# Second expert pair's down weights, and one chunk of the first pair's, loaded as each home comes free

## The chip, the cores and the metric

The kernel runs on one core of a Trainium2 chip. The metric is the device time of one execution in microseconds, lower is better; the time before is the median of three runs.

## The reference

The program is a two-layer graph network on 384 nodes with 1024 features, all in float32. Each layer adds the results of two attention-like mixers to x, normalises, and then adds a mixture of eight experts. The change is in the last stage, the experts of the second layer:

```python
aff = feats @ centroids.T
eid = jnp.argmax(aff, axis=1)
xhat = (feats - mu) * jax.lax.rsqrt(var + EPS)
for e in range(8):
    mask = (eid == e).astype(feats.dtype)[:, None]
    h = xhat * gamma[e] + beta[e]
    y = feats + jax.nn.relu(h @ w1[e] + b1[e]) @ w2[e] + b2[e]
    alpha = jax.nn.sigmoid(feats @ centroids[e])[:, None]
    out = out + mask * (alpha * y + (1.0 - alpha) * feats)
```

Here `w1[e]` is 1024 by 512 and `w2[e]` is 512 by 1024: 2 MB each, 32 MB for eight experts. Each of the 384 rows goes to one expert.

## The kernel before

**Pairs and chunks.** The last stage runs the eight experts as four pairs, 0 to 3; each expert of a pair has 64 of the 128 columns. A pair has sixteen weight chunks of 512 KB (128 partitions of 4 KB): eight up chunks (w1) and eight down chunks (w2). Chunk r of a kind belongs to expert r // 4 of the pair and to step j = r % 4, so step j needs chunks j and 4 + j. `up_pair(i)` (L1573 to L1595, matmuls at L1591) and `down_pair(i)` (L1597 to L1615, matmuls at L1610) work in the four steps j = 0 to 3. TensorE's order is: up of pair 0, up of pair 1, down of pair 0, up of pair 2, down of pair 1, up of pair 3, down of pair 2, the first half of the adding up of results (`spread`, L1630), down of pair 3, and the second half of the adding up. Rows of pairs 1 to 3 are fetched by indirect DMAs (L593) from `xs`, to which ScalarE stores the features (L684); they are turned at L1569. The rows of pair 0 come from SBUF by a matmul with a 0/1 matrix, the first pair's row selection (L1536). The results of pairs 0 and 1 go to `ys` (stored at L862) and come back by three indirect DMAs, and VectorE adds them at L2060. The bias rows b2 of each pair are two broadcast loads (L913).

**Homes.** SBUF is full, so chunks go to tensors that earlier work has finished with. Each of the lists `w1_even`, `w2_even` (pairs 0 and 2), `w1_odd`, `w2_odd` (pairs 1 and 3) names eight homes. Those of `w2_odd` are: three thirds of `Y[:, 3]`, which hold the normalised features of row blocks 0, 1 and 2 and are read last by the first pair's row selection; three thirds of `xnT` (`flat[2]`), which hold the turned features and are read last by the affinity matmuls at L1504, after which the semaphore `pe_output` stands at AFF2; and two thirds of `Y[:, 2]`, which hold the attention's result and are read last by the last matmuls at L1026, after which `chunk_used` stands at CH_F1. The home of chunk 7 of pair 0's down weights is `rows[:, 0]`, which holds a row of factors that VectorE reads last at L2273, just ahead of the L2277 that counts `x2_done` up.

**The order of loads.** SyncE (SP) issues all weight loads from one program, in order: an instruction behind a wait is issued only when the wait is over. Behind the up chunks of pair 1 (into `ring`) it waits for `xn_ready` at 4 * NB (VectorE's L2232, the last of its kind), issues chunk 7 of pair 0's down weights, waits for the row selection (`M1s.xt_ready` at 2) and for the gathered rows of pair 1 (`odd_gathered`), and issues all eight down chunks of pair 1. Behind them come the up chunks of pair 2 (each step's two wait for the same step of pair 0's up), those of pair 3 (wait for pair 1's up), the down chunks of pair 2 (wait for pair 0's down, and for pair 1's down chunks of that step to have landed) and those of pair 3 (wait for pair 1's down, and for pair 2's down chunks of that step to have landed). `load_w2` also waits, for r below 4, until the down chunks of the pair before with the same step have landed (`quarter_in`), which stand on the same semaphore.

Of the kernel before, what the change touches and what calls it, by code (L numbers as in the profile page):

```python
# [31 lines left out]
NB = N // P  # L32
# [14 lines left out]
SLOTS = 8  # L47
# [51 lines left out]
SUMS, MIXED, MIXED2, ALBC, CSUM, AFF, AFF2 = range(1, 8)  # L99
# [58 lines left out]
def program(nc, x, stream, c32, c16, cols_d, edges_d, erows_d, up0_d, dn0_d, wqkv_d, cent_d,  # L158
            bo_g, bo_m, a_lr, gam_d, bet_d, b2_d,
            xs, ys, yo, keys_d, w_lo, w_hi, n_lo, n_hi, out):  # L160
    with ExitStack() as ctx:
        def sb(name, shape, dt=F32):
            return ctx.enter_context(nc.sbuf_tensor(name, shape, dt))

        def sem(name):
            return ctx.enter_context(nc.semaphore(name))
# [6 lines left out]
        Y = sb("Y", [P, 6, KB * N])  # L173
# [100 lines left out]
        pe_output = sem("pe_output")  # L274
        pe_input = sem("pe_input")
        xn_ready = sem("xn_ready")
# [33 lines left out]
        x2_done = sem("x2_done")  # L310
# [62 lines left out]
        def thirds(t):  # L373
            return [t[:, i * 1024:(i + 1) * 1024] for i in range(3)]

        flat = [t[:].rearrange("p a n -> p (a n)") for t in (mask, CT, xnT)]
# [1 line left out]
        w1_even = thirds(Y[:, 4, :]) + [flat[0][:, 0:1024], flat[1][:, 0:1024], Y[:, 5, 1024:2048], g8[1], g8[2]]  # L378
        w2_even = g8[3:7] + [rows[:, 1, :], g8[0], g8[7], rows[:, 0, :]]
        w1_odd = [ring[:, r, :] for r in range(SLOTS)]  # L380
        w2_odd = thirds(Y[:, 3, :]) + thirds(flat[2]) + thirds(Y[:, 2, :])[0::2]
        Xgs = [Xg, g8[8]]
        w1_of, w2_of = [w1_even, w1_odd] * 2, [w2_even, w2_odd] * 2

# [4 lines left out]
        def _(sp):  # L389
# [81 lines left out]
            def load_w1(i, r):  # L471
                if i > 1:
                    sp.wait_ge(landed[r], 16 * (CH_F1 // 8 + i - 1))
                sp.dma_start(w1_of[i][r], stream[CH_F1 + 16 * i + r]).then_inc(landed[r], 16)

            def load_w2(i, r):
                if i and r < 4:
                    sp.wait_ge(quarter_in[r], 16 * NE + 32 * i)
                sp.dma_start(w2_of[i][r], stream[CH_F1 + 16 * i + 8 + r]).then_inc(quarter_in[r % 4], 16)
# [22 lines left out]
            for r in range(SLOTS):  # L502
                sp.wait_ge(chunk_used, CH_F1 - 7 + r)
                load_w1(1, r)
            sp.wait_ge(xn_ready, 4 * NB)
            load_w2(0, 7)
            sp.wait_ge(M1s.xt_ready, 2)
            sp.wait_ge(odd_gathered, 16)
            for r in range(SLOTS):
                load_w2(1, r)  # L510
            for i in range(2, PAIRS):
                for j in range(4):
# [1904 lines left out]
```

## Time and profile before

| | us |
|---|---|
| median of 3 runs (lowest to highest) | 1048.56 (1046.89 to 1048.82) |
| the profiled execution's own time | 1046.18 |
| its span, first to last instruction | 1044.3 |
| TensorE matmul busy | 1011.6 (97%) |
| VectorE busy | 371.4 (36%) |
| GpSimd busy | 318.2 (30%) |
| ScalarE busy | 203.8 (20%) |
| granted clock, mean | 0.992 |

The span is what the profile covers; the own time has 1.88 us more, around it. The profile's starts are counted from the start of the span. TensorE's busy share is high, so what is left to win is in its idle time, which stands in the timeline and in the chain of waits rather than in the busy shares.

### The profile page before, as it was taken

How to read it: one execution, taken by the hardware profiler on the slowest of the kernel's cores; microseconds unless marked ns; L12 is line 12 of the kernel's file. 1: busy time of each engine (PE TensorE's matmuls, PEld its weight loads, DVE VectorE, ACT ScalarE, POOL GpSimd, SP SyncE). 2: the span in 40 equal slices, each digit the busy share in tenths (PEclk: the TensorE clock that was granted, in tenths of full speed). 3: DMA queues.
4: the chain of work that ended last, by engine and by line, in shares of the span. 5: the costliest groups of instructions: out<-in, count | busy, mean ns of one | idle time of the engine just before them, and what ended most of it. 6: DMA issues, size and time to landing. Idle time of an engine off the chain costs nothing.

```text
span 1044.3 us, 10392 instructions
## 1 busy us (share of the span) xinstructions
PE 1011.6 (97%) x3578; PEld 540.8 (52%) x3578; DVE 371.4 (36%) x1043; ACT 203.8 (20%) x418; POOL 318.2 (30%) x246
## 2 busy tenths in 40 slices
PE   6999999999999999999998999999999999999977
PEld 4555555555555545544555665544444455456422
DVE  6034472056200056811155101163102066686314
ACT  3123221111111027820021111111001020012400
POOL 2788887878888830000001000010000000000310
PEclk9999999999999999999998999999999999998999
DMA  9755546544544551013066888771532215653996
GB/s 330 187 101 141 141 101 141 131 111 91 135 103 105 133 191 41 2 56 106 20 230 198 307 321 337 271 285 54 192 100 101 80 41 210 233 176 144 402 365 244
DMA packets 63710, 173.81 MB, mean 166 GB/s; under 512 B 22209, under 2 KB 22945, under 8 KB 63537
## 3 DMA queue, kind: packets, MB, share of 16 engines
q1 hardware_dynamic: 38800, 146.56, 41.3%
q0 software_dynamic: 20816, 15.10, 8.3%
q10 hardware_dynamic: 4048, 11.59, 3.0%
q8 instruction: 24, 0.39, 0.2%
q14 instruction: 22, 0.17, 0.1%
HBM read 161.27 MB, written 11.95 MB: 166 GB/s over the span
## 4 chain that ended last, share of the span: by engine, by line
PE 89%; DMA 5%; DVE 2%; ACT 2%; issue 1%; SPq 0%; ACTq 0%; DVEq 0%; POOL 0%; POOLq 0%
PE bank L1039 36%; PE bank L1050 16%; PE bank L1026 9%; PE bank L1275 7%; PE bank L1300 4%; PE bank L1476 3%; PE bank L1591 2%; DMA rows<-in_stream 2%; PE bank L1140 2%; PE bank L1431 1%; DMA Y<-in_stream 1%; PE bank L1610 1%; PE bank L1126 1%; PE bank L1259 1%; DMA k<-in_c 1%
## 5 line engine op out<-in xcount | busy, mean ns | idle before, releaser
L1039 PE MATMUL bank<-xnT,ring 128*128 128x384 f32 x896 | 292.4, 487 | 1.2 <-ACT xnT L706 1.2
L1039 PEld LDWEIGHTS bank<-xnT,ring 128*128 128x128 f32 x896 | 169.6, 190 | 121.7 <-issue 3.6
L539 POOL DMA_INDIRECT n_lo<-count,ridx x48 | 83.2, 1734 | 16.4 <-issue 14.0
L539 POOL DMA_INDIRECT n_hi<-count,ridx x48 | 81.6, 1701 | 16.9 <-issue 13.7
L593 POOL DMA_INDIRECT Y<-xs,idx x9 | 8.6, 956 | 255.7 <-DMA xs<-xn 178.0
L1050 PE MATMUL bank<-ring,Y 128*128 128x512 f32 x192 | 83.9, 595 | 0.0
L1050 PE MATMUL bank<-ring,xnT 128*128 128x512 f32 x192 | 82.7, 592 | 0.0
L1039 PE MATMUL bank<-Y,ring 128*128 x256 | 82.7, 486 | 0.0
L593 POOL DMA_INDIRECT G<-xs,idx x2 | 2.2, 1122 | 252.7 <-DVE idx L2258 245.0
L1275 PE MATMUL bank<-ring,Y 128*128 128x352 f32 x256 | 77.1, 459 | 0.0
L730 ACT ACTIVATE Y<-bank,sbias,scale 128x384 f32 (+1 forms) x48 | 32.2, 671 | 202.3 <-PE bank L1039 202.3
L1039 PEld LDWEIGHTS bank<-Y,ring 128*128 128x128 f32 x256 | 48.6, 190 | 33.9
L1275 PEld LDWEIGHTS bank<-ring,Y 128*128 128x128 f32 x256 | 48.3, 191 | 25.6 <-issue 0.2
L1050 PEld LDWEIGHTS bank<-ring,Y 128*128 128x128 f32 x192 | 36.1, 190 | 46.1 <-issue 45.8
L1050 PEld LDWEIGHTS bank<-ring,xnT 128*128 128x128 f32 x192 | 36.4, 190 | 45.4 <-issue 45.4
L539 POOL DMA_INDIRECT w_lo<-wts,kidx x48 | 51.8, 1078 | 23.8 <-issue 14.3
L539 POOL DMA_INDIRECT w_hi<-wts,kidx x48 | 53.8, 1120 | 14.6 <-issue 14.6
L1026 PE MATMUL bank<-ring,Y 128*128 128x512 f32 x128 | 56.4, 595 | 0.0
L1026 PE MATMUL bank<-ring,xnT 128*128 128x512 f32 x96 | 41.8, 593 | 0.7 <-ACT xnT L694 0.7
L1710 DVE SCALAR_TENSOR_TENSOR CT<-rows,keyf,k 128x128 bf16<-128x128 f32 x80 | 22.6, 348 | 47.0 <-DMA rows<-keys 46.1
L1791 DVE SCALAR_TENSOR_TENSOR G<-G,mask 128x1152 f32<-128x1152 f32 x1 | 2.0, 2041 | 103.5 <-DMA G<-n_hi 103.5
L1026 PEld LDWEIGHTS bank<-ring,Y 128*128 128x128 f32 x128 | 23.9, 190 | 27.7 <-issue 27.7
(339 smaller groups left out, 1138.2 us busy)
## 6 DMA issues: line engine op xcount, KB each, us to landing
ring<-in_stream SPq DMA_DIRECT2D x144, 512.0 KB, 3.8
ring<-in_up SPq DMA_DIRECT2D x32, 704.0 KB, 5.6
Y<-in_stream SPq DMA_DIRECT2D x18, 512.0 KB, 11.0
G<-in_stream SPq DMA_DIRECT2D x16, 512.0 KB, 7.0
ring<-in_dn SPq DMA_DIRECT2D x7, 1024.0 KB, 5.7
rows<-keys SPq DMA_DIRECT2D x10, 512.0 KB, 6.1
ys<-Y ACTq DMA_DIRECT2D x9, 512.0 KB, 7.3
xnT<-in_stream SPq DMA_DIRECT2D x6, 512.0 KB, 11.2
```

The source lines that it names most:

```text
L539: pool.indirect_dma_start(table, bass.IndirectOffsetOnAxis(ap=at[:, e:e + 1], axis=0), what[:, e:e + 1], None, **how).then_inc(done, 16)
L593: pool.indirect_dma_start(dst, None, src, bass.IndirectOffsetOnAxis(ap=idx[:, col:col + 1], axis=0))\
L730: act.activation(dst, bank[m % 2][:, 0:N], ACT.Identity, bias=bi, scale=sc).then_inc(t_evicted, 1)
L1026: last = pe.matmul(bank[2 + 3 * half + b][:], lhs(2 * (r % 4) + k, b), ring[:, r, k * 512:(k + 1) * 512], start=(start and r == slots[0] a ...
L1039: last = pe.matmul(bank[to][:, 0:N], ring[:, r, k * P:(k + 1) * P], rhs(k), start=(k == 0), stop=(k == KB - 1))
L1050: last = pe.matmul(bank[2 + 3 * half + b][:], lhs(k0 + k, b), ring[:, r, k * 512:(k + 1) * 512], start=(start and k == 0), stop=(stop and ...
L1140: last = pe.transpose(bank[4 + mb][:, b * P:(b + 1) * P], S[:, u, b, mb * P:(mb + 1) * P], ident)
L1275: last = pe.matmul(bank[2 + h][:, 0:F0], x_, W[:, o:o + F0], **se)
L1300: last = pe.matmul(bank[5 + half][:], h_, w_, start=(f == 0), stop=(f == 2))
L1476: last = pe.matmul(bank[2 + r // 4 * 3 + b][:], tok(2)(2 * (r % 4) + k, b), ring[:, r, k * 512:(k + 1) * 512], start=(r % 4 == 0 and k == ...
L1591: last = pe.matmul(bank[2][a * HC:(a + 1) * HC, :], XgT[i % 2][:, 2 * j + k, a * HC:(a + 1) * HC], w1_of[i][4 * a + j][:, k * 512:(k + 1) ...
L1710: last = stt(junk[:, t, :], src, keyf[:, bass.ds(e, 1)], same, ALU.is_equal, ALU.mult, accum_out=ndup[:, bass.ds(e, 1)])
```

## The change

The list of pair 1's (and pair 3's) down homes is put in another order, and the loads of pair 1's down chunks are split into three groups, each with a wait of its own. Chunk 7 of pair 0 waits for `x2_done` in place of `xn_ready`. No load is added or left out.

```diff
-        w2_odd = thirds(Y[:, 3, :]) + thirds(flat[2]) + thirds(Y[:, 2, :])[0::2]
+        y2, y3, t3 = thirds(Y[:, 2, :]), thirds(Y[:, 3, :]), thirds(flat[2])
+        w2_odd = [y2[0], t3[0], t3[2], y3[1], y2[2], t3[1], y3[0], y3[2]]
...
             for r in range(SLOTS):
                 sp.wait_ge(chunk_used, CH_F1 - 7 + r)
                 load_w1(1, r)
-            sp.wait_ge(xn_ready, 4 * NB)
+            for r in (0, 4):
+                load_w2(1, r)
+            sp.wait_ge(x2_done, 4 * NB - 1)
             load_w2(0, 7)
+            sp.wait_ge(pe_output, AFF2)
+            for r in (1, 5, 2):
+                load_w2(1, r)
             sp.wait_ge(M1s.xt_ready, 2)
             sp.wait_ge(odd_gathered, 16)
-            for r in range(SLOTS):
+            for r in (6, 3, 7):
                 load_w2(1, r)
```

## Rows read from the trace of the kernel before

**Rows 1.** Chain of waits, 957 to 1044 us: start, us, what.
```profile
960.20 5.37 PE bank L1591 x24
965.57 1.03 PE bank L1569 x8
...
977.28 6.87 PE bank L1610 x32
...
997.60 21.21 DMA rows<-in_stream
...
1019.25 14.10 DMA Y<-in_stream
```

**Rows 2.** Timeline of TensorE: start, us, instruction, count, idle before and its releaser.
```profile
1006.93 0.59 PE L1610 MATMUL bank<-G,Y 128*64 128x512 f32 x1
...
1011.69 1.94 PE L1610 MATMUL bank<-G,Y 128*64 128x512 f32 x8 [2.87 <-DMA G<-in_stream]
1014.08 1.94 PE L1610 MATMUL bank<-G,Y 128*64 128x512 f32 x8 [0.45 <-DMA G<-in_stream]
1018.86 0.64 PE L1610 MATMUL bank<-G,Y 128*64 128x512 f32 x1 [2.84 <-DMA rows<-in_stream]
...
1020.72 0.66 PE L1285 MATMUL bank<-k,Y 128*128 128x128 f32 x4
...
1027.53 0.64 PE L1610 MATMUL bank<-Y 128*64 128x512 f32 x1
...
1033.39 0.64 PE L1610 MATMUL bank<-xnT,Y 128*64 128x512 f32 x1 [0.49 <-DMA Y<-in_stream]
...
1035.26 5.42 PE L1630 MATMUL bank<-Y 128*128 128x512 f32 x12
```

**Rows 3.** Stretches: us, busy time by engine, TensorE's granted clock, DMA share, GB/s.
```profile
942.00:950.00 8.00, 7.57 (x32) 6.16 (x33) 5.54 (x24) 1.49 (x4) 0.00 (x0) 0.51 0.00 0
957.00:1034.00 77.00, 68.23 (x327) 25.81 (x328) 22.11 (x61) 16.85 (x65) 12.60 (x9) 1.00 0.96 355
970.00:990.00 20.00, 20.00 (x101) 7.43 (x101) 6.72 (x21) 8.30 (x32) 4.83 (x3) 1.00 1.03 412
992.00:996.00 4.00, 4.00 (x22) 1.40 (x20) 0.69 (x1) 0.00 (x0) 0.00 (x0) 1.00 1.05 273
```

**Rows 4.** Timeline of SP's DMA issues, 935 to 1020 us.
```profile
935.92 2.04 SPq L474 DMA_DIRECT2D ring<-in_stream  x2
957.07 0.33 SPq L479 DMA_DIRECT2D rows<-in_stream  x1
961.81 1.53 SPq L479 DMA_DIRECT2D Y<-in_stream  x3
...
964.96 1.04 SPq L479 DMA_DIRECT2D Y<-in_stream  x2
...
979.33 9.25 SPq L474 DMA_DIRECT2D ring<-in_stream  x8
...
997.60 1.08 SPq L522 DMA_DIRECT2D rows<-in_stream  x1
```

**Rows 5.** Timelines of TensorE and VectorE, the last readers of the homes.
```profile
928.79 1.85 PE L1504 MATMUL bank<-cent,xnT 128*128 128x8 f32 x16
...
944.23 3.58 PE L1504 MATMUL bank<-cent,xnT 128*128 128x8 f32 x16
...
941.62 1.41 DVE L2277 SCALAR_TENSOR_TENSOR xr<-Y,rstd,xr 128x512 f32<-128x512 f32 x2
```

**Rows 6.** ScalarE's store of feature block 1 (L684, issued at 934.4 us).
```profile
DMA to landing us min/median/max: 5.4/5.4/5.4
```

**Rows 7.** Timelines of ScalarE's queue, GpSimd and VectorE: store, gather, adding.
```profile
951.68 0.33 ACTq L684 DMA_DIRECT2D xs<-Y  x1
...
956.57 1.30 POOL L593 DMA_INDIRECT G<-xs,idx  x1 [244.97 <-DVE idx L2258]
...
1022.05 3.91 DVE L2060 SCALAR_TENSOR_TENSOR xr<-Y,xr 128x1024 f32<-128x1024 f32 x3
```

## The prediction

> **What bounds the kernel now.** I read the chain of waits first, from its end backwards. Up to 996 us it is TensorE doing one thing after another; then it leaves TensorE for two weight loads: the last down chunk of pair 2 (issued at 997.60, 21.21 us to landing) and the last of pair 3, issued as soon as that one is in (1019.25, 14.10 us, so landed at 1033.35) [rows 1]. A load of 512 KB that takes 14 to 21 us is one that stands in a queue. The stretches say why: from 970 to 990 us the DMA engines' share is 1.03 and they move 412 GB/s, and over the whole of 957 to 1034 us it is 0.96, while from 942 to 950 us they move nothing [rows 3]. So the last 75 us are bound by weight traffic, right behind a stretch in which that resource stood idle.
>
> What that costs TensorE stands in its timeline. Down of pair 2 begins at 1006.93 and is over when L1285 starts at 1020.72: 13.79 us [rows 2], where the same 32 matmul pieces of pair 0 take 6.87 [rows 1]. That is 6.9 us too much. The waits that the timeline names are 2.87 + 0.45 + 2.84 = 6.16; the rest is that the array must refill after each. Down of pair 3 goes from 1027.53 to 1035.26, 7.73 us, 0.86 too much, of which 0.49 is a named wait [rows 2]. So weights cost TensorE 6.16 + 0.49 = 6.65 us by named waits, and 6.9 + 0.9 = 7.8 us by durations. Nothing from 960.20 up to 1006.93 shows such a gap. This 6.65 to 7.8 is all that any change of the loads can give in this stage.
>
> **The change, part by part.**
>
> *Which loads move.* Chunks 0 and 4 of pair 1 now follow the ring loads, the last of which was issued by 937.96 [rows 4]: they go out at about 938.0 and 938.5, at one issue each of some 0.4 us (1.53 for three, 1.04 for two [rows 4]). Chunk 7 of pair 0 waits for the first half of L2277, which starts at 941.62 and takes 1.41 for two: out at about 942.4 in place of 957.07 [rows 4, 5]. Chunks 1, 5 and 2 wait for L1504's end at 944.23 + 3.58 = 947.81: out by 949.2 [rows 5]. Six loads of 0.524 MB, 3.15 MB, leave the crowded stretch. At 412 GB/s they take 3.15 / 0.412 = 7.6 us of the engines, and there is room: 942 to 950 moves 0 GB/s [rows 3]. All six should be in by about 954.
>
> *What is left behind.* Three chunks of pair 1 (6, 3, 7) stay where the eight were, at 961.81 [rows 4], and take some 1.2 us of issue in place of the 4.2 from 961.81 to 966.00 [rows 4]. The up chunks of pair 2, which waited behind them, go out about 3 us sooner as pair 0's up steps end (the 5.37 us from 960.20 cover three of them [rows 1]). Those of pair 3 were issued from 979.33 on for 9.25 us [rows 4], though the ring was free step by step up to 977.28, when pair 1's up is over [rows 1]; they were held by pair 2's landings, and are now held less. The down chunks of pair 2 may go as pair 0's down steps end (977.28 to 984.15 [rows 1]), where the last went out at 997.60. So the queue stays full and the traffic simply ends earlier; I see no point at which a semaphore would starve it, since each group's release comes while at least six chunks of the group before are still in the queue.
>
> *When the last chunk lands.* Two ways. By shift: 1033.35 less 7.6 is 1025.7. By volume: 355 GB/s over 77 us is 27.3 MB [rows 3]; less 3.15 it is 24.2 MB, at the same mean rate 68.1 us, so the end is at 1025.1. TensorE wants it at step 3 of pair 3's down. Without its 6.9 us, that down begins at 1020.6, and step 3 starts three quarters of 6.87 later, at 1025.8 [rows 1, 2]. So the last chunk lands 0.1 to 0.7 us before it is wanted. For pair 2 the last chunk lands at 997.60 + 21.21 = 1018.8 less 7.6, at 1011.2 or before (fewer of the later loads now stand ahead of it), and is wanted at 1006.93 + 5.15 = 1012.1 [rows 1, 2]. Both fit, closely. TensorE's bound (7.8 us) and the traffic's bound (1033.35 less 1025.4, 8.0 us) are nearly the same.
>
> *What is late next.* VectorE's three additions of gathered results (L2060) now end at 1022.05 + 3.91 = 1025.96 [rows 7]. They do not start sooner than their rows arrive, and their DMAs start when they did. The half of the pair-3 result that VectorE takes next is ready at about 1025.8: no room, no loss. Pair 3's bias rows are asked for 7 us sooner, at about 1015, and so fall among the gathers and the last chunks, where they came after them. A stretch with such a pair of broadcast rows moves 273 GB/s against 412 [rows 3]: 4 x (1 - 273 / 412) = 1.3 us of traffic. That loss was there before too, at the very end, where chunks were also landing, so I count it at 0 to 1.3 us. I take 0.6, since half of it was in the old tail.
>
> *What the added waits and early loads may spoil.* SP waits for `x2_done` and AFF2, and nothing else stands behind it that could go before 961.81. The early chunks share the DMA engines with ScalarE's store of feature block 2, which the gathers need. The nearest row is the store of block 1 beside ring loads, 5.4 us [rows 6]. The store of block 2, issued at 951.68, would then be in at 957.1 at worst, while the first gather starts at 956.57 [rows 7]: up to 0.5 us late, hence 962.3 for pair 1's rows in place of just under 961.81 [rows 4], and they are wanted at 965.57 [rows 1]. Cost nothing; without that 3.3 us of cover every us of lateness is a us. Writes of DMA beside TensorE's reading: the 20 us at 412 GB/s have TensorE busy for all 20 [rows 3], so nothing to be charged.
>
> *Sum.* 7.8 by durations and 6.65 by named waits, less 0.6: from 6.05 to 7.2. I take 7.0, near the durations, since they count what the time shows. The profiled execution's span of 1044.3 becomes 1037.3, and its own time of 1046.18 becomes 1039.2. That execution stands 2.4 us under the median of 1048.56; from the median the forecast is 1041.6.
>
> **A rule of the skill that speaks against it.** The row of 970 to 990 us shows 412 GB/s from HBM into SBUF [rows 3]. The Trainium skill, "DMA: Bandwidth & Descriptors", section "Where 436 GB/s comes from", says that for such transfers the HBM side binds, at about 358 GB/s, although it gives a measured 425 for one large load. By 358 the remaining 24.2 MB, of which most now goes at 412, would need some 8 us more, and the last chunk would land no sooner than before: no gain. The trace does not bear that rule out, so it has no share in the chances.
>
> **Rivals.**
>
> *Rival 1, the tail stays with the traffic.* The bias rows of pair 3, the three result gathers and the last chunks are now in the air together. If the 273 GB/s [rows 3] lasts twice as long, 8 us, 2.7 us are lost and the last chunk or the last gathered block is 2 to 3 us late. For: the margins above are 0.1 to 0.9 us. Against: the same pieces crossed before with no more bytes. The gain is about 4, the time 1044.5.
>
> *Rival 2, nothing comes through.* The last chunks wait not for bandwidth but for their semaphores: pair 3's last goes out only when pair 2's has landed, and 14.10 us follow [rows 1]. If each of these waits keeps its place, the freed 7.6 us appear as idle DMA time and the time is 1048.6. Against: a store beside other loads takes 5.4 us, not 14 [rows 6], and the share is 1.03 with no room between.
>
> *Rival 3, slower.* TensorE's clock: just as the loads move, in 942 to 950 us, it stands at 0.51, the 1.2 GHz level, and 16 matmuls of L1504 take 3.58 where they take 1.85 at full clock [rows 3, 5]. If the early traffic makes a feeding step late, the low level could come again in the last stage, where now all is 1.00 [rows 3]. Each us at the low level costs half of it. To end slower than before by the bound below it must lose 7.0 + 2.1 = 9.1 us, so from 18.2 us of low clock on; with 20 us the time is 1051.6. The only idle times here are shorter after the change. The Trainium skill, "TensorE: Matmul & The Clock Gate", Part 1, says that the array is throttled by default and that activity releases it; by that rule fewer waits make this rival less likely.
>
> **How the numbers follow.** Forecast 0.67, rival 1 0.19, rival 2 0.09, rival 3 0.05. What a measurement of this kernel can tell from no change is 0.2%, 2.1 us. Forecast and rival 1 are faster (0.86), rival 2 is the same (0.09), rival 3 slower (0.05). The range: below, a gain of 7.8 with runs as fast as the profiled one gives 1038.4, which I take as seldom and cut at 1039.0; above, it goes over most of rival 1, to 1045.6. Rivals 2 and 3 and the ends left out are about 0.2.
>
> **What would show it.** Right: six loads of L479 issued from 938 to 950 and three at about 962; stretches of 938 to 954 with traffic and an end of the traffic near 1025; no wait at L1610 on a DMA over 0.5 us; down of pair 2 at about 6.9 us. Rival 1 would show a wait at L1610 or L1630 in the last 20 us, on a DMA or on L2060 or L2065. Rival 2 would show DMA shares well under 1 between 990 and 1020. Wrong altogether if TensorE's work up to 1006.93 comes later than before, or the clock is under 1.00 behind 957.

## The result and the profile after

The changed kernel takes 1040.93 us (median of 6 runs, 1036.13 to 1043.46) against 1048.69 us (6 runs, 1046.89 to 1050.02): the ratio is 0.9926 with a 95% interval of 0.9908 to 0.9943, so 6.0 to 9.6 us faster. The forecast was 1041.6, faster, from 1039.0 to 1045.6. A second measurement gave 1042.28 against 1047.90, 0.9937 (0.9913 to 0.9961).

Line numbers of the changed kernel are up to 6 higher: L1616 is the down matmul of before's L1610, L1636 is `spread` (L1630), L1597 is the up matmul (L1591), L2066 is VectorE's addition (L2060).

The profiled execution took 1040.42 us, with a span of 1038.6, which is 5.7 under the 1044.3 of before. It came to the last stage 1.3 us later, so I use one more measure, which is freer of what goes on elsewhere: the **last stage**, from the first matmul of pair 0's up work to the end of the span. Before, it is 1044.3 - 960.20 = 84.1 us [rows 1]; after, 1038.6 - 961.49 = 77.1 us. So 7.0 us are won there.

SP's timeline after (start, us, issue, count), which answers to [rows 4]:

```profile
939.34 2.04 SPq L475 DMA_DIRECT2D ring<-in_stream  x2
941.43 1.08 SPq L480 DMA_DIRECT2D Y<-in_stream  x2
945.83 0.33 SPq L480 DMA_DIRECT2D rows<-in_stream  x1
949.18 1.28 SPq L480 DMA_DIRECT2D xnT<-in_stream  x3
962.83 1.45 SPq L480 DMA_DIRECT2D Y<-in_stream  x3
964.38 0.38 SPq L475 DMA_DIRECT2D Y<-in_stream  x1
```

Six loads are out by 950.5 us and three follow at 962.83, where eight stood. The three wait for the gathered rows. Each is 1.0 to 3.4 us later than forecast because this execution came to this point later: the last matmuls at L1032, ahead of all early loads, end at 941.04, where L1026 ended at 937.61 before.

TensorE's waits from 957 to 1036 us (who waits for whom: total, times, longest):

```profile
PE bank L1597 <- ACT Y L898: 1.3, 1, 1.3
PE bank L1636 <- DVE Y L2030: 0.8, 1, 0.8
PE bank L1616 <- DMA Y<-in_stream: 0.7, 1, 0.7
```

The 6.16 us at pair 2's down [rows 2] are gone. Pair 2's down goes from 1008.22 to 1015.19, where L1291 (L1285 before) starts, 6.97 us in place of 13.79. It begins 46.73 us into the stage, exactly as before (1006.93 - 960.20). Of the waits for weights one is left, 0.7 us where 0.49 stood, at the last step of pair 3's down. The end of the chain of waits (start, us, what) shows it:

```profile
987.50 19.29 DMA rows<-in_stream
...
1007.22 20.79 DMA Y<-in_stream
1028.01 0.04 issue
1028.06 1.94 PE bank L1616 x8
1029.99 5.36 PE bank L1636 x12
```

Compared with [rows 1] the same two loads still end the chain. They are issued 10 and 12 us sooner, and the last takes 20.79 us in place of 14.10: a load still stands as long in the queue, but the traffic starts and ends sooner. The stretches, with the columns of [rows 3]:

```profile
938.00:956.00 18.00, 15.21 (x104) 10.43 (x103) 15.47 (x49) 4.17 (x8) 0.00 (x0) 1.00 0.91 332
956.00:962.00 6.00, 4.69 (x48) 4.20 (x48) 3.11 (x15) 2.58 (x9) 2.06 (x2) 1.00 0.33 100
970.00:990.00 20.00, 20.00 (x110) 8.28 (x109) 7.66 (x23) 7.19 (x29) 6.12 (x3) 1.00 1.02 411
1020.00:1026.00 6.00, 6.00 (x25) 2.01 (x25) 1.76 (x2) 0.00 (x0) 0.00 (x0) 1.00 0.99 281
```

The idle stretch is filled (332 GB/s), a hole stands between it and the last stage (100 GB/s), and the 6 us from 1020, just ahead of the traffic's end at about 1027, run at 281 GB/s. VectorE's timeline shows a second thing that now ends nearly as late as the weights:

```profile
1020.13 1.28 DVE L2066 SCALAR_TENSOR_TENSOR xr<-Y,xr 128x1024 f32<-128x1024 f32 x1 [3.54 <-DMA Y<-ys,idx]
1025.52 1.28 DVE L2066 SCALAR_TENSOR_TENSOR xr<-Y,xr 128x1024 f32<-128x1024 f32 x1 [4.11 <-DMA Y<-ys,idx]
1027.81 1.28 DVE L2066 SCALAR_TENSOR_TENSOR xr<-Y,xr 128x1024 f32<-128x1024 f32 x1 [1.01 <-DMA Y<-ys,idx]
1029.13 0.69 DVE L2071 TENSOR_TENSOR Y<-bank,Y 128x512 f32<-128x512 f32 x1
```

Each of the three additions now waits for its gathered block (before, the three ran in one piece [rows 7]); the first half of pair 3's result (L2071) starts right behind the third, at 1029.13, and is done at 1029.82, 0.17 us before TensorE's L1636 takes it. In the second profile of this kernel (after_again, below) the margin is 0.9 us.

### The profile page after: what moved, and what is told of

It is laid out like the page before. It is cut to its first block, busy times and chain, and to the rows that moved or that the text cites. A ratio compares the mean times of both kernels' runs of the same rounds, so it can differ in the third digit from the quotient of the medians.

```text
span 1038.6 us, 10393 instructions
## 1 busy us (share of the span) xinstructions
PE 1010.6 (97%) x3578; PEld 539.9 (52%) x3578; DVE 372.7 (36%) x1043; ACT 204.0 (20%) x418; POOL 318.5 (31%) x246
## 4 chain that ended last, share of the span: by engine, by line
PE 88%; DMA 6%; DVE 3%; ACT 2%; issue 1%; SPq 0%; ACTq 0%; DVEq 0%; POOL 0%; POOLq 0%
PE bank L1045 36%; PE bank L1056 16%; PE bank L1032 9%; PE bank L1281 7%; PE bank L1306 4%; PE bank L1482 3%; DMA Y<-in_stream 2%; DMA rows<-in_stream 2%; PE bank L1146 2%; PE bank L1437 1%; PE bank L1597 1%; PE bank L1616 1%; PE bank L1132 1%; DMA xs<-xn 1%; PE bank L1265 1%
## 5 line engine op out<-in xcount | busy, mean ns | idle before, releaser
L545 POOL DMA_INDIRECT n_hi<-count,ridx x48 | 81.6, 1700 | 16.3 <-issue 13.7
L1032 PE MATMUL bank<-ring,Y 128*128 128x512 f32 x128 | 56.4, 595 | 0.0
L1032 PE MATMUL bank<-ring,xnT 128*128 128x512 f32 x96 | 41.8, 593 | 0.7 <-ACT xnT L700 0.7
L1032 PEld LDWEIGHTS bank<-ring,Y 128*128 128x128 f32 x128 | 23.9, 190 | 27.7 <-issue 27.7
```

Source lines behind the costliest of these rows:

```text
L545: pool.indirect_dma_start(table, bass.IndirectOffsetOnAxis(ap=at[:, e:e + 1], axis=0), what[:, e:e + 1], None, **how).then_inc(done, 16)
L1032: last = pe.matmul(bank[2 + 3 * half + b][:], lhs(2 * (r % 4) + k, b), ring[:, r, k * 512:(k + 1) * 512], start=(start and r == slots[0] a ...
```

## The experiments

Twelve runs followed the measurement of the change: eleven further kernels and the change once more. The table has, for each, the median against the kernel before measured beside it, the ratio with its interval, and the last stage of its profile (the span's end less the first matmul of pair 0's up). The ratio is estimated from all runs of both kernels, so it isn't always the quotient of the two medians. The stage comes from one profile each; kernels with the same traffic as before gave 83.4 to 85.0 us and the change gave 77.1 and 78.0, so differences in it under about 1 us say little.

| kernel | median us | before us | ratio (95%) | last stage us |
|---|---|---|---|---|
| before | | | | 84.1 |
| e0_homes_only | 1048.96 | 1048.94 | 1.0003 (0.9991 to 1.0015) | 85.0 |
| swap_order_only | 1048.28 | 1048.94 | 1.0002 (0.9984 to 1.0019) | 83.4 |
| e2_two_early | 1046.75 | 1048.94 | 0.9977 (0.9964 to 0.9991) | 81.6 |
| e4_four_early | 1042.43 | 1048.94 | 0.9939 (0.9919 to 0.9960) | 78.6 |
| the change (six early) | 1040.93 | 1048.69 | 0.9926 (0.9908 to 0.9943) | 77.1 |
| after_again | 1042.28 | 1047.90 | 0.9937 (0.9913 to 0.9961) | 78.0 |
| b2_replicated | 1041.46 | 1047.90 | 0.9937 (0.9914 to 0.9960) | 77.4 |
| stored_wait | 1042.20 | 1047.90 | 0.9932 (0.9909 to 0.9955) | 76.5 |
| stored_wait_b2 | 1040.54 | 1047.90 | 0.9928 (0.9906 to 0.9950) | 77.2 |
| b2_one_load | 1040.18 | 1048.35 | 0.9927 (0.9907 to 0.9947) | 76.3 |
| b2_one_stored | 1039.48 | 1048.35 | 0.9921 (0.9899 to 0.9943) | 76.2 |
| b2_left_out | 1040.83 | 1048.35 | 0.9924 (0.9903 to 0.9946) | 76.2 |
| before_b2_one_load | 1044.20 | 1047.58 | 0.9962 (0.9945 to 0.9978) | 78.9 |

**Is it the bytes? A dose.** The first three kernels move 0, 2 and 4 of the six loads, all with the new list of homes.

```diff
 # e0_homes_only: new list, old place
             sp.wait_ge(xn_ready, 4 * NB)
             load_w2(0, 7)
             sp.wait_ge(M1s.xt_ready, 2)
             sp.wait_ge(odd_gathered, 16)
-            for r in range(SLOTS):
+            for r in (0, 4, 1, 5, 2, 6, 3, 7):
                 load_w2(1, r)
 # e2_two_early: 0 and 4 go ahead of the wait for xn_ready
 # e4_four_early: and 1 and 5 too, behind a wait for pe_output at AFF2
```

> The new list of homes, but all nine loads at their old place behind xn_ready and the row selection: no bytes move. Theory T (bytes: the gain is the traffic taken out of the full stretch, 1.27 us for each chunk) expects 0 against before: 1048.7 us, TensorE's waits for weights 6 to 7 us, and 84.1 us from the start of pair 0's up to the end of the span, as before. Rival H (the new homes themselves help, because another step's chunk now stands last in the queue) expects part of the 7.8 us here, over 2.

> Only chunks 0 and 4 of pair 1 go early, behind the ring loads; seven loads stay at their old place. Theory T expects 2 x 1.27 = 2.5 us: 1046.2 us, last stage 81.6 us, named waits for weights about 4 us. A rival by which the gain comes only once the last chunk is in time (all or nothing) expects under 1 us.

> Chunks 0, 4, 1 and 5 of pair 1 go early (two behind the ring loads, two behind the affinities); chunk 7 of pair 0 and four more stay. Theory T expects 4 x 1.27 = 5.1 us: 1043.6 us, last stage 79.0 us, named waits for weights about 1.5 to 2 us. All or nothing expects under 1 us or the whole 7.8.

With none early there is no difference to before by the median, and the stage is 0.9 us longer, so the list of homes gives nothing (rival H falls). Two early give 2.2 us by the medians and 2.5 by the stage, four give 6.5 and 5.5, six give 7.8 and 5.6 in two measurements and 7.0 and 6.1 by the stage. The expected steps were 2.5 and 5.1. So the gain grows with the bytes taken out until TensorE has nearly no waits left, and it is not all or nothing. TensorE's waits for weights in the profile of e2_two_early and of e4_four_early:

```profile
PE bank L1613 <- DMA Y<-in_stream: 2.9, 2, 2.4
...
PE bank L1613 <- DMA rows<-in_stream: 1.3, 1, 1.3
...
PE bank L1613 <- DMA G<-in_stream: 0.2, 1, 0.2
```

```profile
PE bank L1616 <- DMA Y<-in_stream: 2.0, 2, 1.2
```

4.4 us are left with two early and 2.0 with four, of 6.65 before.

**Or the order of issue?** In the kernel before, pair 2's up chunks were put ahead of pair 1's down chunks; no bytes leave the full stretch.

```diff
-            for r in range(SLOTS):
-                load_w2(1, r)
             for i in range(2, PAIRS):
+                if i == 3:
+                    for r in (0, 4, 1, 5, 2, 6, 3, 7):
+                        load_w2(1, r)
                 for j in range(4):
                     sp.wait_ge(M1s.up_used, 4 * i - 7 + j)
```

> The kernel before, with the up chunks of pair 2 issued ahead of the eight down chunks of pair 1: no bytes leave the full stretch, but SP no longer stands in front of pair 2's up chunks with eight issues. Theory T expects no gain, -1 to +0.5 us: 1048.7 us, last stage about 84 us, and the weights' queue as full as before. Rival I (the gain of the change is that the later loads were issued 3 to 6 us sooner, not that there were fewer of them) expects 3 us or more of gain.

Nothing came: 1.0002, with at most 1.7 us inside the interval, and a stage of 83.4. The up chunks of pairs 2 and 3 went out about 4 and 5 us sooner (2.1 and 13.7 us into the stage, where it was 5.9 and 19.1), and pair 1's down chunks about 8 us later. The last two loads, which wait for earlier ones to land, went out only 0.4 and 1.0 us sooner. So another order of the same bytes is worth nothing by itself. In the change the last two go out 11 and 13 us sooner within the stage, and that came only with fewer bytes ahead of them.

**What bounds the rest.** With the change TensorE waits 0.7 to 1.5 us for its last chunk, and the slow stretches stand where the bias rows are loaded. First the changed kernel once more, then three edits on top of it.

> The changed kernel once more, to be compared with the three beside it and for a second profile: 7 to 8 us under before. All theories expect the last stage at 77 us. In its first profile the stretch from the end of L1032 to pair 0's up took 20.5 us at full clock, against 22.6 in before with 10.24 us at the low level. If that is chance, this profile may well show 22.6; if it follows from the change, 20.5 again.

```diff
 # b2_replicated
-  b2_d[2 * i + a].to_broadcast([HC, D])
+  b2_d[2 * i + a, 0:HC, :]           # in HBM each row stands 128 times
 # stored_wait
-            sp.wait_ge(odd_gathered, 16)
+            sp.wait_ge(xs_stored, 96)
```

> The changed kernel, with each expert's bias row laid out 128 times in HBM, so that the two bias loads of a pair read 64 different rows and not one row 64 times; same bytes, same homes. Theory B (reading one row again and again is what brings the engines down to about 270 GB/s wherever these loads run) expects 400 GB/s and more there, some 1.3 us of traffic less for each of three pairs, the last weight and the last gathered block 2 to 4 us sooner against the start of the stage, TensorE's 0.7 us of waiting gone, the stage at 76.3 and 0.8 us less in all. Rival P (they are slow since they write 64 partitions and so load half of the engines' ports) expects no change of the rate and none of the time.

> The changed kernel, with SP waiting for the stored features (xs_stored at 96) in place of the gathered rows (odd_gathered) ahead of its last three chunks. They may then go once the row selection is over, about 2.9 us sooner, into a stretch that moves under 270 GB/s. Theory T expects the last weight about 2 us sooner against the start of the stage (66.5 to 64.5) and the stage 0 to 0.8 us shorter, for TensorE has only 0.7 us of waiting left. The rival (the chunks stand beside the gathers of pairs 1 and 2 and make them late) expects a new wait of TensorE at L1575 of 1 us or more and a slower kernel.

> Both edits together: replicated bias rows and the wait for the stored features. Theory T with B expects no waiting of TensorE on a DMA in the last stage, 76.3 us for it, and no more than the 0.8 us that were left: 1 us under the changed kernel. If more comes, something else than TensorE's waits was bound by the traffic.

Theory B fell. With each partition's row of its own, the stretch with the bias loads of pair 1 is as slow; the first row is of after_again, the second of b2_replicated:

```profile
994.00:996.00 2.00, 2.00 (x12) 0.64 (x10) 0.69 (x1) 0.00 (x0) 0.00 (x0) 1.00 1.04 268
```

```profile
994.00:996.00 2.00, 2.00 (x12) 0.60 (x10) 0.69 (x1) 0.00 (x0) 0.00 (x0) 1.00 1.05 272
```

stored_wait took TensorE's last wait for a weight away and the stage came to 76.5 us, 0.6 to 1.5 less; no wait at the turning of gathered rows appeared. Its chain of waits now ends through the gathered results, not the weights:

```profile
1017.00 12.61 DMA Y<-ys,idx
...
1029.71 1.30 DVE xr L2066
1031.01 0.02 issue
1031.03 0.70 DVE Y L2071
1031.73 0.04 issue
1031.78 5.43 PE bank L1636 x12
```

stored_wait_b2 did not repeat it: 0.8 us of waiting came back and the stage was 77.2. The medians of these four cannot be told apart.

**Half of the partitions.** Next, the two bias loads of a pair, 64 partitions each, became one of 128, whose 128 rows stand in HBM; and, for the bound, the bias rows of pairs 1 to 3 were not loaded at all, so that their experts add pair 0's bias.

```diff
-                for a in range(2):
-                    act.dma_start(b2row[a * HC:(a + 1) * HC, :], b2_d[2 * i + a].to_broadcast([HC, D]))\
-                        .then_inc(b2_in, 16)
+                act.dma_start(b2row, b2_d[i]).then_inc(b2_in, 16)    # [4, 128, D] in HBM
```

> The changed kernel, with the two bias loads of a pair (64 partitions each) made one load of 128 partitions, from a copy in HBM in which each row stands 64 times; same bytes. Theory P (a load of 64 partitions keeps half of the DMA engines' way into SBUF idle, and that makes the 262 to 280 GB/s) expects 400 GB/s and more in these stretches, 1.3 us of traffic less for each of three pairs, the last weight 2 to 3 us sooner against the start of the stage (66.5 to about 64), no wait of TensorE on a weight, and 0.7 to 1.5 us off the stage of 77.1 to 78.0. Rival Q (any load on a second queue beside SP's costs that much) expects nothing.

> The same together with SP's wait for the stored features. Theories T and P expect the last weight at 62 to 63 us from the start of the stage, TensorE waiting for none, the stage at 76.2 to 76.5 us, which is the bound that TensorE's own work sets, and about 1 us under the changed kernel.

> The changed kernel, with the bias rows of pairs 1 to 3 not loaded (pair 0's rows are added for all): 1.57 MB less and no half-width loads in the full stretch. It is the bound for anything done about them. Theories T and P expect the last weight at 61 us or under from the start of the stage and the stage at 76.2 to 76.5; if the stage stays at 77 or over, the traffic was no longer what bound it, and VectorE's additions of gathered rows or TensorE's own order are.

Theory P's numbers come true, and rival Q falls. In b2_one_load the stretches behind the three bias loads run at full rate:

```profile
988.00:994.00 6.00, 6.00 (x30) 2.01 (x28) 0.69 (x1) 1.21 (x5) 0.00 (x0) 1.00 1.03 416
1004.00:1010.00 6.00, 6.00 (x30) 2.01 (x28) 0.69 (x1) 0.00 (x0) 0.07 (x1) 1.00 1.03 414
1012.00:1018.00 6.00, 5.20 (x20) 2.19 (x17) 1.69 (x3) 1.75 (x8) 1.09 (x2) 1.00 1.03 410
```

The DMA queues show what was slowed. First the change (993 to 997 us), then b2_one_load (991 to 996 us); q1 carries the weights, q10 the bias rows (packets, MB, share of the 16 engines' time):

```profile
q1 hardware_dynamic: 162, 0.59, 55.3%
q10 hardware_dynamic: 158, 0.52, 49.7%
```

```profile
q1 hardware_dynamic: 421, 1.54, 76.7%
q10 hardware_dynamic: 159, 0.52, 26.2%
```

A packet of the bias rows takes 0.20 us of an engine in the first and 0.13 in the second, and a packet of the weights beside it 0.22 and 0.15. So the weights' packets are slowed as much as those of the bias rows. The edit changed two things at once: one load in place of two and 128 partitions in place of 64. Which of them counts was not tested apart; that the width does is theory P's reading.

The last weight lands at 1018.4, 58.8 us into the stage, where it was 66.5 and 67.3 in the two profiles of the change, and VectorE and TensorE wait for no load at the end. The chain of waits of its last 36 us is TensorE's own work with one hand-over by VectorE:

```profile
999.52 7.02 PE bank L1593 x32
1006.53 6.89 PE bank L1612 x32
...
1013.45 1.30 DVE Y L2026 x2
...
1014.79 5.42 PE bank L1632 x12
1020.21 7.02 PE bank L1612 x32
1027.23 5.36 PE bank L1632 x12
```

The stage is 76.2 to 76.3 us in b2_one_load, b2_one_stored and b2_left_out alike, and the last of these moves 1.57 MB less. So it is the bound that TensorE's order sets, and less traffic gives no more.

**The same edit where the traffic still binds.** The last kernel has only the one bias load, on the kernel before.

> The kernel before, its loads in their old order, with only the bias rows of a pair made one load of 128 partitions. Theory T (before is bound by traffic in the last stage, and any traffic taken out comes back as time, wherever it is taken) expects the two to three slow stretches of 1.3 us each to come back in full here, 2.6 to 4 us: 1045.5 us, the last stage at 80 to 81.5 us in place of 84.1, where the same edit gave 0.8 to 1.7 us behind the change. The rival (the placing of the nine loads alone decides, through which chunk is last) expects the 0.8 to 1.7 us of there or less, 1047.3 us.

3.4 us by the medians (2.3 to 5.8 by the interval) and a stage of 78.9 us, 5.2 less: more than the 4 of the forecast's upper end by the profile (TensorE's named waits for weights fell by 4.5, from 6.65 to 2.1), and several times the 0.8 to 1.7 that it gives behind the change. That agrees with theory T: traffic time that is taken out of the full stretch comes back as time of the kernel, whether by moving loads or by mending them, until TensorE's 76.2 us are reached. The best of all is b2_one_stored with 1039.48; its interval overlaps with that of the change, and only the stage (76.2 against 77.1 and 78.0) sets them apart.

## Why the prediction was right

**The bound and its size.** The 6.65 to 7.8 us by which the loads held TensorE were the ceiling, by named waits and by durations. The experiments give that ceiling: 84.1 - 76.2 = 7.9 us, with the 84.1 from one profile. Durations agree with it better than named waits: the eight matmuls behind a wait take 1.94 us [rows 2], where eight of the unbroken 32 take 6.87 / 4 = 1.72.

**The sum.** 6.05 to 7.2 was the range, 7.0 the value. The two profiles of the change give 7.0 and 6.1 in the stage. The medians give 7.8 and 5.6; both intervals hold 7.0. That the first median came within 0.7 us of the forecast is in part luck, for the interval is 3.6 us wide and the two terms below were off.

**The signs.** One sign of being right did not come: TensorE's wait for its last chunk was 0.7 and 1.5 us, over the 0.5 of the forecast. One sign of being wrong altogether did come as it is worded: TensorE's work up to pair 2's down came 1.3 us later than before. It came so from the start of the stage on, at an unchanged distance of 46.73 us, and the lateness was there at the end of L1032, before the first early load. So it is a difference between executions, and the sign was badly chosen.

**When the last chunk lands.** This term was mis-sized. The forecast 1025.1 to 1025.7 is 64.9 to 65.5 us into the stage; 66.5 and 67.3 were measured. By shift six chunks should have brought 7.6 us, and brought 6.6 and 5.8. One cause shows in the rows: I counted six chunks out of the full stretch, but chunk 7 had never been in it: it went out at 957.07 [rows 4], ahead of the wait for the gather, when little else moved. Taking it away left a hole: in the six us around the start of the stage 159 GB/s move (957.3 to 963.3 us), where it was 226 before (956 to 962), 0.4 MB less. Five chunks are 5 x 1.27 = 6.4 us, near what was measured; no run moves chunk 7 alone. The 0.6 us for pair 3's bias rows rested on a wrong reading. They did not come behind the last chunks before: this stretch of before has 254 GB/s, ahead of the last landing at 1033.35.

```profile
1028.00:1030.00 2.00, 2.00 (x12) 0.71 (x10) 0.00 (x0) 0.00 (x0) 0.00 (x0) 1.00 1.01 254
```

So no run shows those 0.6 us as a new cost. b2_one_load mends all three slow stretches and shortens the stage by 0.8 to 1.7 us, which is what was left of the ceiling.

**What is late next.** "Their DMAs start when they did" was wrong. The store of pair 1's results landed 48.9 us into the stage in place of 47.6, probably because pair 3's down chunks are now issued right around it, and the gathers began 1.4 us later (50.7 against 49.3) and ended 3.1 us later (66.2 against 63.1). VectorE's first half of pair 3's result did have to wait for the additions, but it was still ready for TensorE, by 0.17 and 0.9 us. So the weights still end last and the gathered rows come close behind; only in stored_wait do the gathered rows end the chain. That is rival 1 in small: 0.8 to 1.7 us over the bound came, not the 3 that it was priced at.

**The cause of 273 GB/s.** I called it a stretch with broadcast rows. That one row is read again and again is not the cause, as b2_replicated shows; two loads of 64 partitions in place of one of 128 are, as b2_one_load shows. The price, 1.3 us for each, held: in windows of 1 us the traffic of the change falls to 12 GB/s at 1027, 65.5 us into the stage, and that of b2_one_load at 1021, 61.4 us into it, so it ends 4.1 us sooner for three such stretches. The last weight lands even 7.7 and 8.5 us sooner (58.8 against 66.5 and 67.3). The part above 4.1 is order within the queue: in b2_one_load the last weight lands 2.6 us ahead of the end of the traffic, in the change 1.0 us behind it. Why the order changed stays open.

**The early loads.** Neither store nor gather suffered. Block 2's store took 3.8 us in place of the 2.9 of before (bound: 5.4), and pair 1's rows were in at 962.8, 4.1 us ahead of their use at 966.86.

**Rivals 2 and 3.** No share of the gain went into idle DMA time behind 962 us, and the clock stood at 1.00 through the last stage. Rival 3's low level stayed ahead of the stage, where it was before: see below. On the limit of 358 GB/s in the Trainium skill, "DMA: Bandwidth & Descriptors", section "Where 436 GB/s comes from": the change ran at 411 GB/s over 20 us and b2_one_load at 416 over 6 us, so the measurement decides against it for this core. The working beside it in the prediction does not hold, though. The forecast's own volume sum used a mean of 355 GB/s, so taking 358 for it changes nothing; the 8 us more stand against a rate of 412 that no sum used.

## What to carry to other kernels

Where the last stage is bound by loads and an idle stretch lies in front of it, count the bytes that can move across the border, and only those that stood in the full queue. Here each 512 KB chunk was worth about 1.3 us until TensorE's own order became the bound, and neither the order of issue nor the choice of homes was worth anything without that. Read a load-bound stage's ceiling from the durations of the same work elsewhere in the kernel, not only from the named waits. Look at GB/s beside the DMA share: here a share of 1.03 at 270 GB/s came from loads of a bad shape, and mending them alone gave 3.4 us where moving six loads gave 7.8 and 5.6.

## What the runs showed of the hardware

Pairs of loads of 64 partitions slowed the weights beside them too: while two of 256 KB ran beside the weight loads, the DMA share stayed at 1.0 and the rate fell to 258 to 281 GB/s, and with one load of 128 partitions and the same bytes it stayed at 410 to 416. That the two loads read one row 64 times each is not the reason: with 64 different rows the rate was 272 where it had been 268.

TensorE's clock stands at its 1.2 GHz level for some 10 us between L1032's end and the last stage in ten of the fourteen profiles, and not in the other four (after, stored_wait_b2, b2_one_load, b2_one_stored). Where it does, the stretch up to pair 0's up work takes 22.3 to 22.7 us, and where it does not 20.4 to 20.5. Rows of after and of after_again:

```profile
944.00:954.00 10.00, 7.70 (x58) 4.89 (x58) 8.76 (x36) 1.70 (x5) 0.00 (x0) 1.00 0.88 327
```

```profile
944.00:954.00 10.00, 9.63 (x47) 7.20 (x48) 7.35 (x31) 1.50 (x5) 0.00 (x0) 0.50 0.67 253
```

These 2.1 us are about a third of the spread of the kernel before (1044.56 to 1051.31 in one measurement). They can also make the median's gain differ from the stage's. The four profiles without the low level have a mean clock of 0.993 or more, the ten with it 0.989 to 0.992. Executions with 0.993 or more were 13 of 48 in the eight measurements with all six loads early, and 9 of 66 in those of the kernel before that stand beside the experiments. Whether the early loads make the full level likelier, or whether this is chance, stays open.
